# The one-hot blocks of a look-up move from VectorE to GpSimd in a fused attention and look-up FFN kernel

## Chip, cores and metric
One core of one Trainium2 chip. The metric is device time in microseconds for one launch of the whole kernel; lower is better. Comparisons in this document are medians of several executions. A difference of about 0.3% (2.1 us here) is the least that a measurement of this kernel can tell from no change.

## What is computed
Two layers, each an attention and a feed-forward part, with residual additions between them. Cut to what matters here (16 batches of 128 rows by 256 columns):

```
# layer 0, attention: 8 heads of 16, over the 256 columns of x[b]
q      = x[b].T @ Wq.T                       # one projection serves as q, k and v
logits = (scale * q q^T masked by columns) * mask of rows     # mask = cond[b]
ctx    = softmax(logits) @ q ;  out0 = ctx @ Wo.T
# layer 0, FFN: its weights are looked up in a table of 16 values
W      = lut[idx]                            # gate 688x256, up 688x256, down 256x688
h      = silu(out0 @ Wgate.T) * (out0 @ Wup.T) ;  x = x + h @ Wdown.T
# layer 1: attention with 16 heads, then a mixture of 4 experts, one expert per row
```

Everything that the change touches lies in the first attention (the first 220 us or so) and in the look-up of the weights `W`, which the kernel does alongside it.

## The kernel before
The kernel is written engine by engine: each engine has its own instruction stream, and semaphores order them. The first attention runs one batch at a time in a software pipeline. In "body i" TensorE (PE) computes the scores of batch i, the transposed scores and contexts of batch i - 1, and the output projection of batch i - 2. Bodies run from 1 to 15 (`LAST`); bodies 3 to 14 are in hardware loops, two bodies to one pass.

The steps of body i that matter:

- **Maxima.** PE writes the scores of a batch in eight pieces into two halves of PSUM bank PB (`scores`, L808). VectorE (DVE) takes the row maxima of each piece (`maximum`, L1231). A piece can be written when the maximum that read its half is done.
- **The turn of the batch.** After the eighth maximum DVE runs `max_columns(i)`: L1238 copies the maxima as bf16 into `mcol`, L1240 writes their low parts (two inputs in SBUF), and L1242 writes the column for absent rows, which doesn't depend on the maxima. PE then transposes `mcol` (`max_rows`, L858), and DVE adds the result to the stacked queries (`add_max`, L1247). PE's transposed scores of the batch (L820) wait for that addition, so nothing of the next body but one piece of scores and one projection can run before it.
- **One-hot blocks.** The look-up is done by matmuls (L847): a block of 32 x 128 indices is spread over 128 partitions by a DMA from `idx_low` (`load_hot`, L544, issued by ScalarE at the start of body i for block i, 1 MB written), compared with each partition's value (`one_hot`, L1220 in the trace, 128x4096 bf16, output again 0 or 1 in bf16), and multiplied by the table. There are 17 blocks (`LCH`). In the kernel before DVE does `one_hot(i - 1)` between `max_columns(i)` and `add_max(i)`. Blocks 15 and 16 have no body of their own and come after body 15; the load of block 16 waits for `one_hot(14)`, and the FFN waits for the last look-up (`w0` reaching `LCH`).
- **Context.** DVE normalises the context of batch i - 2 in four steps, L1253, L1256, L1259 (two inputs in SBUF) and L1266, which signals `ct`. PE projects it (L865), ScalarE copies it out (L534), and GpSimd splits it into high and low bf16 parts (`context_parts`, L381 and L384).
- **GpSimd (POOL).** Once PE has placed batch i + 1 (`pq`), GpSimd makes the product of x and mask for batch i + 2 (`projected`: L389, two inputs, and the copy L391). Then it waits for the context of batch i - 2 and splits it. Between bodies 13 and 14 it issues ten DMAs with weights for the second layer (L426, L427).

Of the kernel before, what the change touches and what calls it, by code (L numbers as in the profile page):

```python
# [10 lines left out]
ALU = mybir.AluOpType  # L11
# [31 lines left out]
LCH = -(-LUSED // LCOLS)  # L43
# [7 lines left out]
ROW_MAX, ROW_MAX_LOW, ROW_ABSENT = 3, 7, 11  # L51
# [3 lines left out]
C_V = C_ROWS + SLOTS  # L55
# [25 lines left out]
def program(nc, x, cond, condT, consts, wqT, woT, lut, idx_all, w_emb, b_emb, g_norm, w_qkv, g_q, g_k,  # L81
            w_out, w_outT, w_r, b_r, w_all, out, tok_x, tok_r, idx_low):
    with ExitStack() as ctx:
        def sb(name, shape, dt=F32):
            return ctx.enter_context(nc.sbuf_tensor(name, shape, dt))
# [8 lines left out]
        cst = sb("cst", [P, C_N])  # L94
# [17 lines left out]
        def bf(*shape):  # L112
            n = int(np.prod(shape)) // 2
            v = arena[:, at[0]:at[0] + n].bitcast(BF16)
            at[0] += n
            return v
# [20 lines left out]
        spread = bf(2, LHOT).rearrange("p (a c) -> p a c", a=2)  # L137
        hot = bf(2, LHOT).rearrange("p (a c) -> p a c", a=2)
# [21 lines left out]
        def part(shape, dt=F32):  # L160
            n = int(np.prod(shape[1:])) * (1 if dt == F32 else 2) // (1 if dt == F32 else 4)
            v = small[:, small_at[0]:small_at[0] + n]
            small_at[0] += n
            assert small_at[0] <= SMALL
            if dt != F32:
                v = v.bitcast(dt)
            names = "abcd"[:len(shape) - 1]
            if len(names) == 1:
                return v
            return v.rearrange(f"p ({' '.join(names)}) -> p {' '.join(names)}", **dict(zip(names, shape[1:])))  # L170
# [15 lines left out]
        nmax = sb("nmax", [P, PAIRS, 2, KT])  # L186
        mcol = part([P, KT, PAIRS, P], BF16)
# [84 lines left out]
        S = {}  # L272
# [17 lines left out]
        def unless_first(engine, semaphore, count):  # L290

            if not (isinstance(count, int) and count <= 0):
                engine.wait_ge(semaphore, count)

        def hot_rows(c):

            return idx_low[:, bass.ds(c * LHOT, LHOT)].unsqueeze(1).broadcast_to([LG, LUT, LHOT])

        block = ctx.enter_context(nc.Block())
        LAST = B - 1  # L300
        U = B // 2
# [69 lines left out]
        def _(pool):  # L371
# [5 lines left out]
            def context_parts(b):  # L377
                pool.wait_ge(S["c"], b + 1)
                o = bass.ds(b * P, P)
                c32 = c_out.rearrange("p (k t) -> p k t", k=KT)  # L380
                nc.gpsimd.tensor_tensor(c_hi[:, :, o], c32, wz[:].unsqueeze(2).broadcast_to([P, KT, P]), ALU.add  # L381
                                        ).then_inc(S["ch"], 1)
                pool.wait_ge(S["ch"], b + 1)
                nc.gpsimd.tensor_tensor(c_lo[:, :, o], c32, c_hi[:, :, o], ALU.subtract).then_inc(S["cl"], 1)  # L384


            def projected(b, par, half):
                pool.wait_ge(S[f"mk{par}"], 16 * half + 16)
                nc.gpsimd.tensor_tensor(xm[:, par, :].unsqueeze(1), xall[:, bass.ds(b, 1), :], mk[:, par, :].unsqueeze(1),  # L389
                                        ALU.mult).then_inc(S["xm"], 1)  # L390
                nc.gpsimd.tensor_copy(present[:, par, :], mk[:, par, :]).then_inc(S["present"], 1)  # L391

            def body(i, par, half, before=True, after=True):
                if after:
                    pool.wait_ge(S["pq"], 2 * i + 2)
                    projected(i + 2, par, half)
                if before:
                    context_parts(i - 2)

            pool.wait_ge(S["x"], 16)  # L400
            projected(0, 0, 0)
            projected(1, 1, 0)
            nc.gpsimd.memset(vu[:], 1.0).then_inc(S["ones"], 1)
            pool.wait_ge(S["idx"], 16)
# [6 lines left out]
            pool.wait_ge(S["idxs"], 16)  # L411
            for c in range(2):
                pool.dma_start(spread[:, c, :], hot_rows(c)).then_inc(S[f"hot_first{c}"], 16)
            body(1, 1, 1, before=False)
            pool.wait_ge(S["x_rest"], 16)
            body(2, 0, 2)
            with pool.Fori(1, U - 2) as u:
                body(2 * u + 1, 1, u + 1)
                body(2 * u + 2, 0, u + 2)
            body(LAST - 2, 1, U - 1)  # L420
            for dst, src in ((wemb[:], w_emb.rearrange("(k p) n -> p k n", p=P)), (bemb[:], b_emb), (gnorm[:], g_norm),
                             (gqk[:, 0, :], g_q.broadcast_to([P, DK1])), (gqk[:, 1, :], g_k.broadcast_to([P, DK1])),
                             (w2[:, :, 0:T], w_out.rearrange("(k p) n -> p k n", p=P)),
# [1 line left out]
                             (wr[:], w_r.rearrange("(k p) n -> p k n", p=P)), (br[:], b_r.broadcast_to([P, E]))):  # L425
                pool.dma_start(dst, src).then_inc(S["small3"], 16)  # L426
            pool.dma_start(wqkv[:], w_qkv.rearrange("(k p) n -> p k n", p=P)).then_inc(S["wqkv"], 16)  # L427
            body(LAST - 1, 0, 0, after=False)
            body(LAST, 1, 0, after=False)
            context_parts(LAST - 1)  # L430
            context_parts(LAST)

# [751 lines left out]
        def _(dve):  # L1184
            v = nc.vector
# [25 lines left out]
                                    ).then_inc(S["lutw"], 1)  # L1211


            def one_hot(c, par, half):
                if isinstance(c, int) and c < 2:
                    dve.wait_ge(S[f"hot_first{c}"], 16)
                else:
                    dve.wait_ge(S[f"hot{par}"], 16 * half)
                unless_first(dve, S["lmm"], c - 1)
                v.tensor_scalar(hot[:, par, :], spread[:, par, :], cst[:, C_V:C_V + 1], None, ALU.is_equal).then_inc(S["onehot"], 1)  # L1220

            def low(b):
                dve.wait_ge(S["ph"], b + 1)
                unless_first(dve, S["pq"], 2 * b)
                v.tensor_tensor(pl[:], PA[:, 0:T], ph[:], ALU.subtract).then_inc(S["pl"], 1)

            def maximum(b, c, s):
                dve.wait_ge(S["sa"], 8 * b + 2 * c + s + 1)
                if c == s == 0:
                    unless_first(dve, S["mc"], 3 * b)  # L1230
                v.tensor_reduce(nmax[:, c, s, :], PB[:, s * 512:(s + 1) * 512].rearrange("p (a k) -> p a k", k=T),  # L1231
                                AX.X, ALU.max, negate=True).then_inc(S["max"], 1)

            def max_columns(b):
                dve.wait_ge(S["max"], 8 * b + 8)
                unless_first(dve, S["mt"], b)
                cols = mcol.rearrange("p q r (s m) -> p r s q m", s=2)
                v.tensor_copy(cols[:, :, :, :, ROW_MAX], nmax[:]).then_inc(S["mc"], 1)  # L1238
                dve.wait_ge(S["mc"], 3 * b + 1)
                v.tensor_tensor(cols[:, :, :, :, ROW_MAX_LOW], nmax[:], cols[:, :, :, :, ROW_MAX], ALU.subtract).then_inc(S["mc"], 1)  # L1240

                v.tensor_copy(mcol[:, :, :, ROW_ABSENT::64].rearrange("p q r s -> p q (r s)"),  # L1242
                              nbig[:, :, bass.ds(b, 1)].broadcast_to([P, KT, 2 * PAIRS])).then_inc(S["mc"], 1)

            def add_max(b, par):
                dve.wait_ge(S["mt"], b + 1)
                v.tensor_tensor(qs[:, par, :], PD[:, 512:1024].bitcast(BF16), qs[:, par, :], ALU.add).then_inc(S["q2"], 1)  # L1247
# [20 lines left out]
            def body(i, par, half, before=True, after=True):  # L1268
                if before:
                    normalise(i - 2, 0)  # L1270
                maximum(i, 0, 0)
                if before:
                    normalise(i - 2, 1)
                    normalise(i - 2, 2)
                maximum(i, 0, 1)
                if before:
                    normalise(i - 2, 3)
                if after:
                    low(i + 1)
                maximum(i, 1, 0)  # L1280
                maximum(i, 1, 1)
                maximum(i, 2, 0)
                maximum(i, 2, 1)
                maximum(i, 3, 0)
                maximum(i, 3, 1)
                max_columns(i)
                one_hot(i - 1, 1 - par, half)
                add_max(i, par)

            dve.wait_ge(S["kprep"], 1)  # L1290
            low(0)
            low(1)
            for c in range(4):
                for s in range(2):
                    maximum(0, c, s)
            max_columns(0)
            add_max(0, 0)
            table()
            body(1, 1, 0, before=False)
            body(2, 0, 0)  # L1300
            with dve.Fori(1, U - 1) as u:
                body(2 * u + 1, 1, u)
                body(2 * u + 2, 0, u)
            body(LAST, 1, U - 1, after=False)
            for n in range(4):
                normalise(LAST - 1, n)
            for c in range(LAST, LCH):
                one_hot(c, c % 2, c // 2)
            for n in range(4):
                normalise(LAST, n)  # L1310

# [384 lines left out]
```

## Time and profile before

| | us |
|---|---|
| median of 3 runs | 706.95 |
| lowest and highest | 706.39 and 708.73 |
| the profiled execution | 707.92 |
| its span in the trace | 706.2 |

| engine | busy in the span |
|---|---|
| TensorE matmul | 580.7 us, 82% |
| VectorE | 419.2 us, 59% |
| ScalarE | 326.3 us, 46% |
| GpSimd | 118.9 us, 17% |

Durations in the trace come from the one profiled execution, which took 0.97 us more than the median. Busy shares are means over stages with different limits; within the first attention DVE is busy for most of each batch and GpSimd for about a fifth of it.

### The profile page before, as it was taken

What the parts mean: (1) busy time and instruction counts of PE and PEld (TensorE: products, weight loads), DVE (VectorE), ACT (ScalarE), POOL (GpSimd) and SP (SyncE); (2) the same over time, 40 slices, a digit from 0 to 9 for tenths busy, and PEclk for the clock granted to TensorE, in tenths of its full rate; (3) what the DMA queues carried; (4) which work ended last, traced back from release to release, by engine and by line L of the source; (5) the groups of instructions that cost most, each with busy time, mean ns of one, the idle gap of its engine ahead of it and who ended that gap; (6) DMA issues with size and microseconds to landing.
All of it is one profiled execution on the core that took longest, in us unless ns stands there. A gap on an engine that the chain in (4) does not pass through costs nothing.

```text
span 706.2 us, 15569 instructions
## 1 busy us (share of the span) xinstructions
PE 580.7 (82%) x5115; PEld 347.5 (49%) x5147; DVE 419.2 (59%) x943; ACT 326.3 (46%) x592; POOL 118.9 (17%) x161
## 2 busy tenths in 40 slices
PE   3798989899976999995688777775199999999992
PEld 1344445455534655552354554443156666666661
DVE  1678698989853334343799999996523333333330
ACT  2456667677752332342677777773022222222220
POOL 4221122121511000000000000000203333322211
PEclk9999899999986999997799999997599999999996
DMA  8844345454851000005556666551101111011110
GB/s 295 202 95 113 90 110 123 113 121 108 156 134 32 1 1 0 0 0 125 159 120 150 149 147 148 132 137 46 24 22 46 45 45 41 31 37 37 45 32 3
DMA packets 29413, 60.27 MB, mean 85 GB/s; under 512 B 5989, under 2 KB 16647, under 8 KB 26952
## 3 DMA queue, kind: packets, MB, share of 16 engines
q1 hardware_dynamic: 20624, 25.68, 12.4%
q0 software_dynamic: 6432, 18.46, 12.2%
q10 hardware_dynamic: 2328, 15.75, 9.6%
q8 instruction: 18, 0.29, 0.2%
q14 instruction: 11, 0.09, 0.0%
HBM read 58.75 MB, written 7.81 MB: 94 GB/s over the span
## 4 chain that ended last, share of the span: by engine, by line
PE 27%; DVE 14%; issue 7%; ACT 3%; DVEq 1%; DMA 0%; POOL 0%; POOLq 0%; ACTq 0%
PE PA L1134 8%; PE PD L1153 7%; PE PB L1134 7%; PE PC L1142 2%; DVE arena L1479 2%; DVE small L1451 1%; ACT small L661 1%; DVE ms L1405 1%; DVE newt L1373 1%; PE PB L1020 1%; DVE rs L1379 1%; DVE newt L1376 1%; DVE small L1433 1%; DVE small L1437 1%; PE PD L1122 1%
## 5 line engine op out<-in xcount | busy, mean ns | idle before, releaser
L1231 DVE TENSOR_REDUCE nmax<-PB 128x2 f32<-128x512 f32 x128 | 85.5, 681 | 27.0 <-PE PB L808 25.4
L529 ACT ACTIVATE probs<-PC 128x512 f32<-128x512 f32 x128 | 73.9, 609 | 21.6 <-PE PC L820 20.6
L737 ACT CAST probs<-PC 128x1024 bf16<-128x1024 f32 x19 | 19.2, 1012 | 113.7 <-PE PC L1142 113.7
L1625 DVE TENSOR_TENSOR probs<-PC,probs 128x1024 bf16<-128x1024 f32 x19 | 23.3, 1225 | 80.9 <-ACT probs L737 80.9
L1134 PE MATMUL PA<-arena,probs 128*128 x227 | 53.7, 387 | 7.6 <-issue 3.8
L808 PE MATMUL PB<-small 64*128 64x256 bf16 x256 | 52.4, 297 | 8.2 <-DVE nmax L1231 6.1
L1153 PE MATMUL PD<-arena,probs 128*128 x456 | 54.5, 277 | 2.5 <-issue 2.5
L820 PE MATMUL PC<-small 64*128 64x256 bf16 x256 | 48.1, 289 | 3.8 <-DVE small L1247 3.5
L1153 PEld LDWEIGHTS PD<-arena,probs 128*128 128x128 bf16 x456 | 45.0, 99 | 9.0 <-issue 3.2
L1134 PE MATMUL PB<-arena,probs 128*128 x210 | 48.6, 379 | 0.9
L444 POOL DMA_DIRECT2D arena<-in_w_all x16 | 8.5, 532 | 236.7 <-DVE arena L1479 139.5
L669 ACT ACTIVATE probs<-PA,gb 128x1024 f32<-128x1024 f32 x32 | 35.6, 1113 | 14.7 <-PE PA L1047 14.7
L834 PE MATMUL PD<-probs,vu 128*32 128x256 f32 x512 | 38.6, 424 | 4.5 <-ACT probs L529 2.4
L1134 PEld LDWEIGHTS PA<-arena,probs 128*128 128x128 bf16 x228 | 22.4, 99 | 34.8 <-issue 14.5
L466 POOL DMA_INDIRECT out<-probs,tokn x19 | 19.3, 1016 | 118.2 <-DVE probs L1632 118.2
L1348 DVE TENSOR_TENSOR wst<-PB,wst 128x512 f32<-128x512 f32 (+1 forms) x24 | 16.6, 690 | 34.8 <-PE PB L972 26.5
L972 PE MATMUL PA<-arena 128*128 (+1 forms) x133 | 34.2, 389 | 1.9 <-ACT arena L539 1.1
L1020 PE MATMUL PB<-wqkv,small 128*128 128x512 f32 x64 | 34.0, 657 | 2.1 <-ACT small L640 2.1
L972 PE MATMUL PB<-arena 128*128 (+1 forms) x143 | 35.4, 382 | 0.1
L1134 PEld LDWEIGHTS PB<-arena,probs 128*128 128x128 bf16 x228 | 22.3, 98 | 22.9
L1479 DVE TENSOR_TENSOR arena<-wst,arena 128x512 f32 (+1 forms) x48 | 32.6, 682 | 0.0
L381 POOL TENSOR_TENSOR arena<-wst,wz 128x256 f32 (+1 forms) x16 | 9.8, 613 | 133.5 <-ACT wst L534 133.5
(201 smaller groups left out, 1163.9 us busy)
## 6 DMA issues: line engine op xcount, KB each, us to landing
arena<-idx_low ACTq DMA_DIRECT2D x15, 1024.0 KB
wst<-in_w_all SPq DMA_DIRECT2D x48, 256.0 KB, 2.7
arena<-in_w_all POOLq DMA_DIRECT2D x16, 384.0 KB, 5.9
arena<-in_idx_all SPq DMA_DIRECT2D x1, 2176.0 KB, 10.1
arena<-in_cond SPq DMA_DIRECT2D x16, 128.0 KB, 9.3
small<-in_x SPq DMA_DIRECT2D x16, 128.0 KB, 10.0
arena<-idx_low POOLq DMA_DIRECT2D x2, 1024.0 KB, 14.9
tok_r<-rows SPq DMA_DIRECT2D x1, 2048.0 KB, 14.4
```

What stands on the lines that cost most here:

```text
L529: nc.scalar.activation(probs[:, c, o], PC[:, o], ACT.Exp, scale=SCALE0).then_inc(S["ex"], 1)
L669: nc.scalar.activation(probs[:, 2 * par + c, :], PA[:], ACT.Exp, scale=DK1 ** -0.5, bias=gb[:]).then_inc(S["e3"], 1)
L808: ins = mm(PB[:, s * 512 + qt * T:s * 512 + (qt + 1) * T], qs[r, par, c * T + qt * P:c * T + (qt + 1) * P], ks[r, par, c * T:(c + 1) * T], ...
L820: ins = mm(PC[:, s * 512 + n * T:s * 512 + (n + 1) * T], ks[r, par, pr * T + kt * P:pr * T + (kt + 1) * P], qs[r, par, pr * T:(pr + 1) * T ...
L834: ins = mm(PD[h * HS:(h + 1) * HS, pp * T:(pp + 1) * T], vu[:, par, kt, GROUP * pp + h, :], probs[:, pp * KT + kt, o:o + T], start=(kt == ...
L972: ins = mm(o, w0(w, which, kt, m), v[:, kt, tok], start=(k == 0), stop=(k == 3 * KT - 1))
L1020: ins = mm(PB[:, 0:512], xnT[:, kt, :], wqkv[:, kt, 0:512], start=(kt == 0), stop=(kt == KT - 1))
L1134: ins = mm(bank[:, n * 512:(n + 1) * 512], v[:, par, xo], w[:, o], start=(k == 0), stop=(k == 3 * KT - 1))
L1153: ins = mm(PD[:, 512:512 + T], v[:, f * P:(f + 1) * P], w[:, o], start=(k == 0), stop=(k == 3 * FT - 1))
L1231: v.tensor_reduce(nmax[:, c, s, :], PB[:, s * 512:(s + 1) * 512].rearrange("p (a k) -> p a k", k=T), AX.X, ALU.max, negate=True).then_inc( ...
L1479: v.tensor_tensor(all_lo[:, o], wst[:, n, par * SUB:(par + 1) * SUB], all_hi[:, o], ALU.subtract).then_inc(S[f"wsl{n}"], 1)
L1625: v.tensor_tensor(hT_lo, PC[:], hT_hi, ALU.subtract).then_inc(S["hTl"], 1)
```

## The change
`one_hot` moves from DVE to GpSimd. In body i GpSimd now first waits for the loaded block i - 1 and for `ct` of batch i - 2 (the end of DVE's normalising in this body); then it makes `projected(i + 2)`, then `one_hot(i - 1)`, then `context_parts(i - 2)`. Blocks 15 and 16 are made by GpSimd too, ahead of the last two `context_parts`. On DVE the copy for absent rows moves ahead of the eighth maximum (which moves into `max_columns`), and `add_max` follows `max_columns` directly. The comparison itself, its operands and its size stay the same.

```diff
+            def hot_ready(c, par, half):
+                if isinstance(c, int) and c < 2:
+                    pool.wait_ge(S[f"hot_first{c}"], 16)
+                else:
+                    pool.wait_ge(S[f"hot{par}"], 16 * half)
+                unless_first(pool, S["lmm"], c - 1)
+            def one_hot(c, par):
+                nc.gpsimd.tensor_scalar(hot[:, par, :], spread[:, par, :], cst[:, C_V:C_V + 1], None, ALU.is_equal).then_inc(S["onehot"], 1)
...
-            def body(i, par, half, before=True, after=True):
+            def body(i, par, half, hot, before=True, after=True):
+                hot_ready(i - 1, 1 - par, hot)
+                if before:
+                    pool.wait_ge(S["ct"], i - 1)
                 if after:
                     pool.wait_ge(S["pq"], 2 * i + 2)
                     projected(i + 2, par, half)
+                one_hot(i - 1, 1 - par)
                 if before:
                     context_parts(i - 2)
...
+            for c in range(LAST, LCH):
+                hot_ready(c, c % 2, c // 2)
+                one_hot(c, c % 2)
             context_parts(LAST - 1)
             context_parts(LAST)
...
             def max_columns(b):
-                dve.wait_ge(S["max"], 8 * b + 8)
+                cols = mcol.rearrange("p q r (s m) -> p r s q m", s=2)
                 unless_first(dve, S["mt"], b)
-                cols = mcol.rearrange("p q r (s m) -> p r s q m", s=2)
-                v.tensor_copy(cols[:, :, :, :, ROW_MAX], nmax[:]).then_inc(S["mc"], 1)
-                dve.wait_ge(S["mc"], 3 * b + 1)
-                v.tensor_tensor(cols[:, :, :, :, ROW_MAX_LOW], nmax[:], cols[:, :, :, :, ROW_MAX], ALU.subtract).then_inc(S["mc"], 1)
-
                 v.tensor_copy(mcol[:, :, :, ROW_ABSENT::64].rearrange("p q r s -> p q (r s)"),
                               nbig[:, :, bass.ds(b, 1)].broadcast_to([P, KT, 2 * PAIRS])).then_inc(S["mc"], 1)
+                maximum(b, 3, 1)
+                dve.wait_ge(S["max"], 8 * b + 8)
+                v.tensor_copy(cols[:, :, :, :, ROW_MAX], nmax[:]).then_inc(S["mc"], 1)
+                dve.wait_ge(S["mc"], 3 * b + 2)
+                v.tensor_tensor(cols[:, :, :, :, ROW_MAX_LOW], nmax[:], cols[:, :, :, :, ROW_MAX], ALU.subtract).then_inc(S["mc"], 1)
...
                 maximum(i, 3, 0)
-                maximum(i, 3, 1)
                 max_columns(i)
-                one_hot(i - 1, 1 - par, half)
                 add_max(i, par)
...
             for n in range(4):
                 normalise(LAST - 1, n)
-            for c in range(LAST, LCH):
-                one_hot(c, c % 2, c // 2)
             for n in range(4):
                 normalise(LAST, n)
```

## Rows read from the trace of the kernel before

**Rows 1.** Timeline, turn of batch 10: start us, duration us, engine, line, operation, [idle before]

```profile
144.67 0.69 DVE L1231 TENSOR_REDUCE nmax<-PB 128x2 f32<-128x512 f32 x1 [0.74 <-PE PB L808]
...
145.37 1.07 PE L834 MATMUL PD<-probs,vu 128*32 128x256 f32 x16
145.40 0.20 DVE L1238 CAST small<-nmax 128x16 bf16<-128x16 f32 x1
145.60 0.73 POOL L389 TENSOR_TENSOR small<-arena 128x256 f32<-128x256 f32 x1 [0.87 <-PE PA L792]
145.64 0.77 DVE L1240 TENSOR_TENSOR small<-nmax,small 128x16 bf16<-128x16 f32 x1
...
146.27 0.40 POOL L391 CAST arena<-arena 128x256 bf16<-128x256 f32 x1
146.29 0.43 DVE L1242 CAST small<-nbig 128x16 bf16 x1
146.61 1.27 DVE L1220 TENSOR_SCALAR arena<-arena,cst 128x4096 bf16<-128x4096 bf16 x1
146.78 0.62 PE L858 MATMUL PD<-identb,small 128*128 128x128 bf16 x8 [0.34 <-DVE small L1242]
...
147.81 0.68 DVE L1247 TENSOR_TENSOR small<-PD,small 128x1024 bf16<-128x1024 bf16 x1
```

**Rows 2.** Timeline, the part of body 10 ahead of that turn

```profile
136.51 0.68 DVE L1247 TENSOR_TENSOR small<-PD,small 128x1024 bf16<-128x1024 bf16 x1
...
139.53 0.44 DVE L1266 STREAM_TRANSPOSE wst<-small 128x256 f32<-128x256 f32 x1
...
142.42 1.51 DVE L1231 TENSOR_REDUCE nmax<-PB 128x2 f32<-128x512 f32 x2 [0.28 <-PE PB L808]
...
143.25 0.61 POOL L381 TENSOR_TENSOR arena<-wst,wz 128x256 f32 x1 [7.87 <-ACT wst L534]
```

**Rows 3.** Timeline, turn of batch 15, with no GpSimd work beside it

```profile
199.93 1.07 PE L834 MATMUL PD<-probs,vu 128*32 128x256 f32 x16 [0.88 <-ACT probs L529]
...
200.94 0.62 PE L858 MATMUL PD<-identb,small 128*128 128x128 bf16 x8
...
201.59 0.69 DVE L1247 TENSOR_TENSOR small<-PD,small 128x1024 bf16<-128x1024 bf16 x1
```

**Rows 4.** GpSimd by line: shapes, count | busy us, mean ns | idle before, releasers

```profile
L384 POOL TENSOR_TENSOR arena<-wst,arena 128x256 f32 (+1 forms) x16 | 10.7, 671 | 2.4 <-POOL arena L381 1.9
L381 POOL TENSOR_TENSOR arena<-wst,wz 128x256 f32 (+1 forms) x16 | 9.8, 613 | 133.5 <-ACT wst L534 133.5
...
L391 POOL CAST arena<-arena 128x256 bf16<-128x256 f32 x16 | 6.4, 399 | 0.0
L405 POOL CAST arena<-arena 128x4352 bf16<-128x4352 int32 x1 | 3.8, 3811 | 3.6 <-DMA arena<-in_idx_all 3.6
```

**Rows 5.** Timeline, turn of batch 0

```profile
23.97 0.41 DVE L1238 CAST small<-nmax 128x16 bf16<-128x16 f32 x1
...
25.61 1.01 PE L858 MATMUL PD<-identb,small 128*128 128x128 bf16 x8 [2.41 <-DVE small L1242]
```

**Rows 6.** Line L413, loads of blocks 0 and 1: duration min/median/max, first and last start

```profile
L413 POOL DMA_DIRECT2D arena<-idx_low x2: 613/650/687, 23.0 to 23.7; - x2
...
DMA to landing us min/median/max: 13.7/14.9/16.1
```

**Rows 7.** One batch: window, length, busy PE, PEld, DVE, ACT, POOL, clock, DMA share, GB/s

```profile
64.22:80.31 16.09, 14.40 (x137) 7.34 (x137) 10.32 (x19) 8.41 (x16) 2.36 (x4) 0.68 0.35 89
```

**Rows 8.** Timeline, end of the first attention and the last blocks

```profile
178.12 0.80 POOL L426 DMA_DIRECT2D wemb<-in_w_emb  x1
...
180.97 0.64 ACTq L544 DMA_DIRECT2D arena<-idx_low  x1
...
217.69 1.29 DVE L1220 TENSOR_SCALAR arena<-arena,cst 128x4096 bf16<-128x4096 bf16 x1 [7.39 <-DMA arena<-idx_low]
...
219.04 1.02 PE L847 MATMUL PD<-lutw,arena 128*128 128x16 bf16 x32 [4.49 <-DVE arena L1220]
```

More of the change, by code:

```diff
@@ L396, in body @@
                     projected(i + 2, par, half)
+                one_hot(i - 1, 1 - par)
                 if before:
                     context_parts(i - 2)
+            pool.wait_ge(S["cst"], 16)
             pool.wait_ge(S["x"], 16)
@@ L413, in _ @@
                 pool.dma_start(spread[:, c, :], hot_rows(c)).then_inc(S[f"hot_first{c}"], 16)
-            body(1, 1, 1, before=False)
+            body(1, 1, 1, 0, before=False)
             pool.wait_ge(S["x_rest"], 16)
-            body(2, 0, 2)
+            body(2, 0, 2, 0)
             with pool.Fori(1, U - 2) as u:
-                body(2 * u + 1, 1, u + 1)
-                body(2 * u + 2, 0, u + 2)
-            body(LAST - 2, 1, U - 1)
+                body(2 * u + 1, 1, u + 1, u)
+                body(2 * u + 2, 0, u + 2, u)
+            body(LAST - 2, 1, U - 1, U - 2)
             for dst, src in ((wemb[:], w_emb.rearrange("(k p) n -> p k n", p=P)), (bemb[:], b_emb), (gnorm[:], g_norm),
@@ L427, in _ @@
             pool.dma_start(wqkv[:], w_qkv.rearrange("(k p) n -> p k n", p=P)).then_inc(S["wqkv"], 16)
-            body(LAST - 1, 0, 0, after=False)
-            body(LAST, 1, 0, after=False)
+            body(LAST - 1, 0, 0, U - 2, after=False)
+            body(LAST, 1, 0, U - 1, after=False)
+            for c in range(LAST, LCH):
+                hot_ready(c, c % 2, c // 2)
+                one_hot(c, c % 2)
             context_parts(LAST - 1)
@@ L1211, in table @@
                                     ).then_inc(S["lutw"], 1)
[L1214 to L1220, printed above, removed]
             def low(b):
@@ L1292, in _ @@
             low(1)
-            for c in range(4):
-                for s in range(2):
-                    maximum(0, c, s)
+            for n in range(7):
+                maximum(0, n // 2, n % 2)
             max_columns(0)
```

## The prediction, made before the changed kernel was run
> **What bounds the kernel now.** I read the timeline of one ordinary batch first, since the busy shares don't say which wait ends last. Body 10 runs from one `add_max` to the next, 136.51 to 147.81, 11.30 us [rows 1, 2]; below, t counts from its start. DVE is nearly always busy, but idles 0.74 us ahead of the eighth maximum, waiting for PE [rows 1]. After that maximum (t = 8.16 to 8.85) comes a chain of single steps: L1238, L1240, L1242, PE's `max_rows` at 146.78 (t = 10.27), and `add_max` at t = 11.30.
>
> Two costs sit in this chain. **First**, L1240 and L1242, 16 elements each, take 0.77 and 0.43 us. L1240 ends just after GpSimd's L389 ends (146.41 and 146.33), L1242 just after L391 ends (146.72 and 146.67): DVE stands still while GpSimd works, and gets in as each GpSimd instruction ends [rows 1]. **Second**, `one_hot` on DVE ends at 147.88, so `add_max` starts 1.03 us after `max_rows` did; where nothing stands in the way it starts 0.65 us after it (200.94 to 201.59) [rows 1, 3].
>
> PE sets a floor under both. `max_rows` stands behind 16 context matmuls, which hold PE's queue for 1.01 us (199.93 to 200.94) [rows 3]. In body 10 they start at t = 8.86 [rows 1], so `max_rows` can't start before t = 9.87, nor `add_max` before 10.52. At most 0.8 us of 11.30 is to be had, not the 1.27 us of the removed instruction. Bodies 13 to 15 have no products of x and mask and nearly stand there: block 14's load, issued as body 14 starts, and `add_max` of batch 15 are two batches and 20.6 us apart [rows 3, 8].
>
> **What the moved comparison costs on GpSimd.** No row shows it. The nearest are GpSimd's one-input casts: 128x256 in 0.399 us, 128x4352 in 3.811 us [rows 4], which is 3.412 / 4096 = 0.833 ns an element and 0.19 us fixed. For 4096 elements: 3.6 us. The other end is the two-input rows: L381 (613 - 186) / 256 = 1.67 ns an element, so 7.0 us; L384 (671 - 186) / 256 = 1.89 ns, so 7.9 us [rows 4]. Below 1.27 us, DVE's own time [rows 1], I exclude. I take 3.6: the comparison has one input in columns (the other is one value a partition), as the casts do, and L405 has almost its length.
>
> **The body after.** GpSimd now waits for `ct`, the end of L1266 at t = 3.46 [rows 2], plus 0.19, what L384 waits for L381 (1.9 us over 10) [rows 4]. Behind that wait stand the products, the comparison and the split of the context. The products take 0.73 and 0.40 us, overlapping by 0.06 [rows 1]: t = 3.65 to 4.7. PE wants them only in the next body, and SP's next mask load only half a body later, so this delay costs nothing. The comparison runs t = 4.7 to 8.3. L381 and L384 follow, 0.61, 0.19 and 0.67 us: to t = 9.8 (before they began at t = 6.74 [rows 2]). ScalarE needs that buffer again a batch later: no cost.
>
> DVE meets this in two places. L1242, now ahead of the eighth maximum, is due at t = 7.42 (142.42 + 1.51) [rows 2]; without contention it would hide in the 0.74 us of idling. The comparison holds it to 8.3, so the eighth maximum starts at 8.35 instead of 8.16 and ends at 9.05. Then L1238 and L1240 (0.20 and 0.23 us free) meet L384, t = 9.1 to 9.8: whichever goes first, L1240 ends near 10.0. `max_rows` starts at 10.1 and `add_max` 0.65 later, 10.75. Against 11.30 (its neighbours are about 11.2) that is **0.5 us a batch**, where the floor allows 0.8.
>
> **The sum.** Turns 2 to 12 have the products beside them now: 11 x 0.5 = 5.5 us, of which I give batch 4, at a lower clock, the same. Turn 0: L1238 ends at 24.38; with L389 and L391 waiting for block 0, `max_rows` starts at 24.38 + 0.04 + 0.23 + 0.06 = 24.7 instead of 25.61: 0.9 us [rows 5]. Block 0 lands near 23.0 + 13.7 = 36.7 [rows 6], its comparison then runs from 37.8 to 41.4, and the turn of batch 1 falls there; I take L1238 and L1240 as just ahead of it, at nothing; if they lose, 2 us. Body 13 loses 0.3 us (10.75 instead of 10.4). So body 14 begins 0.9 + 5.5 - 0.3 = 6.1 us earlier, and load 14 with it.
>
> Now the end. Block 16's comparison waited 7.39 us for its DMA, until 217.69, and the last look-up follows at 219.04 [rows 8]; the FFN waits for that. The stream of loads 14 to 16, mixed with the ten weight DMAs that GpSimd issues from 178.12, sets the end, not the engines. Load 14 (180.97) leaves 6.1 us earlier. The weight DMAs stand behind body 13's comparison and leave 2 us later within their body (t = 9.8 instead of 7.8), so 6.4 - 2.0 = 4.4 us earlier. With both kinds sharing the DMA engines the last block lands between: 5.3 us earlier. In body 14 the comparison stands behind the ten issues and holds the turn by some 2 us; that cover is the same DMA wait. At the end the comparison of block 16 takes 3.6 - 1.3 = 2.3 us longer with nothing beside it. Net 5.3 - 2.3 = **3.0 us**. The profiled execution (707.92, of which 706.2 is span) would be 704.9; it is 0.97 above the median, so 706.95 - 3.0 = **703.9 us**.
>
> A rule of the Trainium skill speaks of the stall: "SBUF — State Buffer", section "Who interferes with whom", says that a GpSimd instruction and a VectorE instruction with two SBUF inputs or in a two-port mode exclude each other for the whole instruction. The trace agrees, with 0.77 us for 16 elements [rows 1]. By it L1242 would be held up to 3.6 us if it came as the comparison started, while the maxima, which read PSUM, would run on.
>
> **Rivals.**
>
> *The comparison is slow on GpSimd, and DVE waits for it (slower).* If it runs at the two-input rate, 7.0 us, it ends at t = 11.7; L1242 and with it the eighth maximum are held until then, and `add_max` comes 2.45 us after its end, as in my reckoning (8.3 to 10.75), at t = 14.15. Each us above 3.6 costs 1 us in each of bodies 2 to 13 and about half of one at the end, 12.5 in all. It decides from 3.6 + 3.0 / 12.5 = 3.84 us: slower beyond that, and measurably from 4.0. At 5 us the time is 703.9 + 17.5 = 721.4, at 7.0 us 703.9 + 42.5 = 746.4. For it: no row shows a comparison on GpSimd, and two-input rows are twice as slow an element. Against: the one-input casts of two types and lengths lie on one line. "GPSIMD Engine Reference" of the Trainium skill, section 7, points the same way as this rival: loops that compare and then select need 2.03 cycles an element unless unrolled, 1.03 if they are; at its 1.2 GHz an estimate of 6.9 us or 3.5 us.
>
> *The gain is lost at the end (no change).* If the weight DMAs alone decide when block 16 lands, and turn 1 loses its race with block 0's comparison (2 us), what is left is 4.4 - 2.0 - 2.3 = 0.1 us: 706.9. For it: the tail already waits for DMAs, and any gain of the batches has to pass them. Against: load 14 is issued with the batch, not by GpSimd.
>
> *Batch 4 keeps its clock (faster still).* That batch takes 16.09 us with a granted clock of 0.68, partly at 1.2 instead of 2.4 GHz, against 11.3 for others [rows 7]. If the new timing spares it that drop, 4.8 us more come off: 699.1. The same chance cuts the other way if a drop comes elsewhere.
>
> **How the numbers follow.** My forecast 0.50 (its own range 701.5 to 706.5, by the races at the turns and the DMA mix; of it 0.36 are faster by over 0.3%, about what a measurement of this kernel can tell from no change). Slow comparison 0.28, nearly all slower. Lost at the end 0.12, mostly no change. The clock 0.10, mostly faster. That gives faster 0.44, same 0.23, slower 0.33. The range runs from 699 to 722: below it little is left, above it the comparison over 5 us, 0.15 or so.
>
> **What would show it.** The comparison's row on GpSimd, near 3.6 us, decides most. L1242 should end with the comparison, near t = 8.3; L1240 should end near 10.0, `max_rows` should follow at 10.1 and `add_max` 0.65 later; the batches should be 10.7 to 10.8 us apart. The last comparison should start near 212.4 and the last look-up near 216.1. I am wrong if the comparison is longer than 3.8 us, if DVE's instructions lose more than one race a turn, or if block 16 lands less than 4 us earlier.

## The result: 14.5% slower, and the profile after

The changed kernel takes 806.66 us (median of 4 runs, 802.85 to 812.12) against 706.67 us; the ratio is 1.145, 95% interval 1.139 to 1.151. Its profiled execution took 812.12 us, of which 810.0 is span. Each later experiment has runs of the kernel before made beside it: 29 with a median of 707.34 (702.25 to 711.99) for the experiments 1 to 3, 7 with 707.71 for 5 and 6, and 11 with 707.74 for 4 and for the repeated run in 3. A ratio leaves out executions over 1.5% above the fastest of their kernel, which are two of the ten in experiment 2 and none elsewhere.

Nearly all of it lies in the first attention: the last look-up starts at 317.41 instead of 219.04 [rows 8], 98.4 us later, of 103.8 between the two spans. The other 5.4 us lie behind it, in an execution that was itself 5.5 above the median of its kernel. The two costliest groups there, from the page of the changed kernel (line engine op, shapes, count | busy us, mean ns | idle before), and its row of granted clock in 40 slices:

```profile
L394 POOL TENSOR_SCALAR arena<-arena,cst 128x4096 bf16<-128x4096 bf16 x17 | 180.6, 10624 | 4.9 <-DVE wst L1275 4.9
...
L1246 DVE CAST small<-nbig 128x16 bf16 (+1 forms) x16 | 79.6, 4978 | 0.0
...
PEclk9998555686566565999997799999856999999997
```

The comparison takes **10.62 us** on GpSimd, where VectorE took 1.27 [rows 1]. And a copy of 16 elements, L1246 (L1242 before), takes 4.98 us in the mean. The timeline of body 7 shows how they belong together; it answers to [rows 1, 2]. (`add_max` is L1256 now, the maxima L1240, the end of normalising L1275, the two steps behind the eighth maximum L1250 and L1252.)

```profile
138.38 0.69 DVE L1256 TENSOR_TENSOR small<-PD,small 128x1024 bf16<-128x1024 bf16 x1 [1.13 <-PE PD L875]
...
141.64 0.44 DVE L1275 STREAM_TRANSPOSE wst<-small 128x256 f32<-128x256 f32 x1
...
142.52 0.73 POOL L398 TENSOR_TENSOR small<-arena 128x256 f32<-128x256 f32 x1 [4.74 <-DVE wst L1275]
...
143.57 10.63 POOL L394 TENSOR_SCALAR arena<-arena,cst 128x4096 bf16<-128x4096 bf16 x1
143.57 0.69 DVE L1240 TENSOR_REDUCE nmax<-PB 128x2 f32<-128x512 f32 x1 [0.17 <-PE PB L825]
...
148.99 5.26 DVE L1246 CAST small<-nbig 128x16 bf16 x1
...
152.41 1.85 DVE L1240 TENSOR_REDUCE nmax<-PB 128x2 f32<-128x512 f32 x1
154.17 0.62 POOL L381 TENSOR_TENSOR arena<-wst,wz 128x256 f32 x1
154.32 0.53 DVE L1250 CAST small<-nmax 128x16 bf16<-128x16 f32 x1
...
154.88 0.23 DVE L1252 TENSOR_TENSOR small<-nmax,small 128x16 bf16<-128x16 f32 x1
...
155.17 0.62 PE L875 MATMUL PD<-identb,small 128*128 128x128 bf16 x8 [3.09 <-DVE small L1252]
...
155.82 0.69 DVE L1256 TENSOR_TENSOR small<-PD,small 128x1024 bf16<-128x1024 bf16 x1 [0.71 <-PE PD L875]
```

What is to be seen: the comparison runs from 143.57 to 154.20, that is t = 5.2 to 15.8. L1246 starts at 148.99 and ends at 154.25, 0.05 us after the comparison, though it has 16 elements a partition. The next `add_max` follows at t = 17.44, against 11.30 before. In most batches it is 17.88: there TensorE, which now idles for about 3 us in a turn, has fallen to its 1.2 GHz level, and `max_rows` lasts 1.03 instead of 0.62 us. The maximum behind L1246 has a record of 1.85 us that overlaps with L1246 and ends within 0.01 us of it. So the time of the maximum did not come on top of the wait.

Where the 98.4 us are, by the starts of `add_max` in both traces: the turn of batch 1 comes 7.3 us later (48.74 against 41.46; the first two rows below), batches 2 to 11 add 60.1 (226.42 against 159.02), batches 12 to 15 add 28.4 (297.38 against 201.59), and the end 2.6. There two comparisons run back to back, and the last look-up waits for GpSimd instead of for the DMA [rows 8]:

```profile
38.63 10.62 POOL L394 TENSOR_SCALAR arena<-arena,cst 128x4096 bf16<-128x4096 bf16 x1
38.73 8.88 DVE L1252 TENSOR_TENSOR small<-nmax,small 128x16 bf16<-128x16 f32 x1
...
284.23 10.61 POOL L394 TENSOR_SCALAR arena<-arena,cst 128x4096 bf16<-128x4096 bf16 x1 [4.88 <-DVE wst L1275]
...
296.15 21.20 POOL L394 TENSOR_SCALAR arena<-arena,cst 128x4096 bf16<-128x4096 bf16 x2
...
317.41 1.02 PE L864 MATMUL PD<-lutw,arena 128*128 128x16 bf16 x32 [1.57 <-POOL arena L394]
```

### The profile page after: what moved, and what is told of

It reads as the page before. It is cut to its first block and busy times, and to the rows that moved or that the text cites. A ratio compares the mean times of both kernels' runs of the same rounds, so it can differ in the third digit from the quotient of the medians.

```text
span 810.0 us, 15559 instructions
## 1 busy us (share of the span) xinstructions
PE 645.8 (80%) x5115; PEld 371.6 (46%) x5147; DVE 484.7 (60%) x926; ACT 333.5 (41%) x592; POOL 297.2 (37%) x178
## 5 line engine op out<-in xcount | busy, mean ns | idle before, releaser
L394 POOL TENSOR_SCALAR arena<-arena,cst 128x4096 bf16<-128x4096 bf16 x17 | 180.6, 10624 | 4.9 <-DVE wst L1275 4.9
L1240 DVE TENSOR_REDUCE nmax<-PB 128x2 f32<-128x512 f32 x128 | 103.3, 812 | 47.2 <-PE PB L825 45.4
L1246 DVE CAST small<-nbig 128x16 bf16 (+1 forms) x16 | 79.6, 4978 | 0.0
L825 PE MATMUL PB<-small 64*128 64x256 bf16 x256 | 71.6, 387 | 1.3 <-DVE nmax L1240 1.3
L837 PE MATMUL PC<-small 64*128 64x256 bf16 x256 | 62.7, 387 | 1.0 <-DVE small L1256 1.0
L875 PE MATMUL PD<-identb,small 128*128 128x128 bf16 x128 | 15.3, 293 | 52.4 <-DVE small L1252 52.4
L851 PE MATMUL PD<-probs,vu 128*32 128x256 f32 x512 | 49.8, 526 | 4.4 <-ACT probs L546 2.4
L523 ACT CAST ph<-PA 128x256 bf16<-128x256 f32 x16 | 6.0, 372 | 93.7 <-PE PA L788 88.1
L686 ACT ACTIVATE probs<-PA,gb 128x1024 f32<-128x1024 f32 x32 | 35.6, 1113 | 15.3 <-PE PA L1064 15.3
L875 PEld LDWEIGHTS PD<-identb,small 128*128 128x128 bf16 x128 | 11.4, 132 | 61.6 <-DVE small L1252 59.7
L398 POOL TENSOR_TENSOR small<-arena 128x256 f32<-128x256 f32 x16 | 11.7, 730 | 73.3 <-DVE wst L1275 54.4
```

The source lines that it names most:

```text
L394: nc.gpsimd.tensor_scalar(hot[:, par, :], spread[:, par, :], cst[:, C_V:C_V + 1], None, ALU.is_equal).then_inc(S["onehot"], 1)
L686: nc.scalar.activation(probs[:, 2 * par + c, :], PA[:], ACT.Exp, scale=DK1 ** -0.5, bias=gb[:]).then_inc(S["e3"], 1)
L825: ins = mm(PB[:, s * 512 + qt * T:s * 512 + (qt + 1) * T], qs[r, par, c * T + qt * P:c * T + (qt + 1) * P], ks[r, par, c * T:(c + 1) * T], ...
L837: ins = mm(PC[:, s * 512 + n * T:s * 512 + (n + 1) * T], ks[r, par, pr * T + kt * P:pr * T + (kt + 1) * P], qs[r, par, pr * T:(pr + 1) * T ...
L851: ins = mm(PD[h * HS:(h + 1) * HS, pp * T:(pp + 1) * T], vu[:, par, kt, GROUP * pp + h, :], probs[:, pp * KT + kt, o:o + T], start=(kt == ...
L875: ins = pe.transpose(M[:, pr * T + qt * P:pr * T + (qt + 1) * P], mcol[:, qt, pr, :], identb[:])
```

## Experiment 1: what makes the comparison so slow

Behind the last store of the kernel before, GpSimd runs nine operations one after the other, each waiting for the one ahead. (A step that fills the f32 inputs with ones comes first and isn't shown.) `cv` is the column of one value a partition.

```diff
+step(g.tensor_scalar(hot[:, 0, :], spread[:, 0, :], cv, None, ALU.is_equal))
+step(g.tensor_scalar(hot[:, 0, 0:2048], spread[:, 0, 0:2048], cv, None, ALU.is_equal))
+step(g.tensor_scalar(hot[:, 0, 0:1024], spread[:, 0, 0:1024], 3.0, None, ALU.is_equal))
+step(g.tensor_scalar(hot[:, 0, 0:512], spread[:, 0, 0:512], cv, None, ALU.mult))
+step(g.tensor_scalar(fout[:, 0:2048], fin[:, 0:2048], cv, None, ALU.is_equal))
+step(g.tensor_copy(hot[:, 0, :], spread[:, 0, :]))
+step(g.tensor_tensor(hot[:, 0, 0:1536], spread[:, 0, 0:1536], spread[:, 1, 0:1536], ALU.mult))
+step(g.tensor_tensor(fout[:, 0:1536], fin[:, 0:1536], fin[:, 1536:3072], ALU.mult))
+step(g.tensor_scalar(fout[:, 0:1792], fin[:, 0:1792], cv, None, ALU.mult))
```

> The kernel before, with ten GpSimd instructions added one after the other behind its last store: the moved comparison again (4096 columns of bf16), the same at 2048, the comparison against a constant (1024), a multiplication by the same column of cst (512 bf16, 1792 f32), the comparison in f32 (2048), a plain copy (4096 bf16) and two-input products (1536 bf16, 1536 f32). Theory A, the comparison itself is slow: it takes 2.5 to 2.6 ns an element at every size, type and kind of scalar, the multiplications by a column and the copy stay at the cast's 0.83. Theory B, any instruction with a scalar is slow on GpSimd: the multiplications take 2.5 ns too. Theory C, bf16 is slow: the f32 comparison is at 0.83 and the bf16 copy at 2.5. The time is some 30 to 45 us above that of before and of no interest.

Timeline of that run, GpSimd alone:

```profile
701.04 10.64 POOL L500 TENSOR_SCALAR arena<-arena,cst 128x4096 bf16<-128x4096 bf16 x1
711.77 5.43 POOL L501 TENSOR_SCALAR arena<-arena,cst 128x2048 bf16<-128x2048 bf16 x1
717.29 2.77 POOL L502 TENSOR_SCALAR arena<-arena 128x1024 bf16<-128x1024 bf16 x1
720.16 1.58 POOL L503 TENSOR_SCALAR arena<-arena,cst 128x512 bf16<-128x512 bf16 x1
721.83 5.44 POOL L504 TENSOR_SCALAR arena<-arena,cst 128x2048 f32<-128x2048 f32 x1
727.34 3.60 POOL L505 COPY arena<-arena 128x4096 bf16<-128x4096 bf16 x1
731.02 3.08 POOL L506 TENSOR_TENSOR arena<-arena 128x1536 bf16<-128x1536 bf16 x1
734.18 3.42 POOL L507 TENSOR_TENSOR arena<-arena 128x1536 f32<-128x1536 f32 x1
737.69 4.80 POOL L508 TENSOR_SCALAR arena<-arena,cst 128x1792 f32<-128x1792 f32 x1
```

**Theory B holds.** It is one execution, but each instruction starts within 0.1 us of the end of the one ahead, so the starts give the same lengths. From 4096 and 2048 columns: 5.21 / 2048 = 2.54 ns an element and 0.22 us fixed. A multiplication (512 and 1792 columns), an immediate in place of the column (1024), and f32 all lie on that line within 0.1 us. The plain copy of the same 4096 elements takes 3.60 us, exactly what the prediction took for the comparison. So the kind of instruction sets the rate: the operations with a scalar that were tried (is_equal and a product) cost GpSimd three times a copy an element, and more than a product of two tensors (1.9 to 2.1 ns, with the copy's fixed 0.19 us taken off). "GPSIMD Engine Reference" of the Trainium skill, section 4.1, calls one-input operations on GpSimd roughly line rate. The copy agrees (0.83 ns), the operation with a scalar doesn't; the measurement decides. That comparing is what costs, which section 7 would have suggested, is refuted: the multiplication is as slow.

## Experiment 2: the same design with the cost that was predicted

```diff
-nc.gpsimd.tensor_scalar(hot[:, par, :], spread[:, par, :], ...)
+nc.gpsimd.tensor_scalar(hot[:, par, 0:1344], spread[:, par, 0:1344], ...)
```

The blocks are also set to zero once at the start (not shown). Everything beyond column 1344 is left out, so this kernel computes something else and serves only for its time.

> The changed kernel with the comparison cut to its first 1344 of 4096 columns (the other columns of the blocks stay zero, so most of the looked-up weights are left out); the look-up's matmuls and all waits are as they were. At 2.55 ns an element it takes 3.6 us, what the prediction took for the whole. Theory 1, only the size of that term was wrong: 703.9 (701.5 to 706.5), batches 10.7 to 10.8 us apart, add_max some 2.45 us after the end of the comparison. Theory 2, a comparison beside VectorE costs more than its length, by the exclusion of each other's SBUF accesses: above 707, batches over 11.3 us apart.

Measured: 707.4 us (10 runs, 699.87 to 711.88), ratio 0.998 (0.994 to 1.002). The comparison takes 3.69 us. Timeline of body 9 of this run:

```profile
120.66 0.69 DVE L1258 TENSOR_TENSOR small<-PD,small 128x1024 bf16<-128x1024 bf16 x1 [0.93 <-PE PD L877]
...
125.63 3.69 POOL L395 TENSOR_SCALAR arena<-arena,cst 128x1344 bf16<-128x1344 bf16 x1
...
128.01 1.37 DVE L1248 CAST small<-nbig 128x16 bf16 x1
128.76 0.69 DVE L1242 TENSOR_REDUCE nmax<-PB 128x2 f32<-128x512 f32 x1
...
130.45 0.62 PE L877 MATMUL PD<-identb,small 128*128 128x128 bf16 x8
...
131.11 0.69 DVE L1258 TENSOR_TENSOR small<-PD,small 128x1024 bf16<-128x1024 bf16 x1 [0.87 <-PE PD L877]
```

Inside the first attention theory 1 holds in that the comparison costs no more than its length, and the batch is even shorter than forecast: 10.45 and 10.52 us in turn instead of 10.75, TensorE's floor. `add_max` follows 1.8 us behind the comparison (129.32 to 131.11), not 2.45. The copy (here L1248) is held to 129.38, but the maximum behind it starts at 128.76 as soon as TensorE has the scores. The FFN's first matmul (of the group in PA) starts 5.7 us earlier than before (215.42 against 221.14). Yet the whole is not faster, and as a time both theories missed: 707.4 lies above the range of the one, and its batches are far below those of the other. In the profiled execution all but 1.2 us of the gain is gone within 45 us of the start of the FFN, whose granted clock is lower (columns as in [rows 7]; the kernel before has 0.90 and 1.00 in its first two such windows):

```profile
214.00:234.00 20.00, 18.87 (x106) 11.07 (x106) 6.71 (x19) 5.89 (x9) 3.10 (x5) 0.77 0.01 1
234.00:254.00 20.00, 18.48 (x102) 10.12 (x102) 6.94 (x12) 5.35 (x9) 0.00 (x0) 0.91 0.01 1
```

The kernels of experiments 3 and 4 keep their gain. Why this one doesn't was not settled. That most of its looked-up weights are zero is not enough for it: in experiment 4 a kernel with nearly all of them zero keeps its gain, with a granted clock of 0.89 and 1.00 in the same two stretches of its FFN (207 to 227 and 227 to 247).

## Experiment 3: the second part of the change by itself

The change also delays the products of x and mask until VectorE has normalised the context. Here that alone, with the comparison left on VectorE, and then with the new order of the copy as well.

```diff
             def body(i, par, half, before=True, after=True):
+                if before:
+                    pool.wait_ge(S["ct"], i - 1)
                 if after:
                     pool.wait_ge(S["pq"], 2 * i + 2)
                     projected(i + 2, par, half)
```

> The kernel before with one wait added: GpSimd makes the products of x and mask only after ct, as in the changed kernel; the comparison stays on VectorE. Theory 1, L1240 and L1242 stand still for the products: they fall to 0.23 and 0.20 us in all turns, add_max comes 0.7 us earlier in 11 of them, and the time is 699 (698 to 701). Theory 2, the floor of TensorE and the comparison on VectorE eat it: 705 to 707.

Measured: 700.39 us (12 runs, 695.74 to 705.58), ratio 0.990 (0.987 to 0.993). Timeline of a turn of this run:

```profile
140.81 0.68 DVE L1249 TENSOR_TENSOR small<-PD,small 128x1024 bf16<-128x1024 bf16 x1
...
149.63 0.21 DVE L1240 CAST small<-nmax 128x16 bf16<-128x16 f32 x1
149.87 0.23 DVE L1242 TENSOR_TENSOR small<-nmax,small 128x16 bf16<-128x16 f32 x1
149.97 0.21 DVE L1244 CAST small<-nbig 128x16 bf16 x1
150.16 1.29 DVE L1222 TENSOR_SCALAR arena<-arena,cst 128x4096 bf16<-128x4096 bf16 x1
151.37 0.68 DVE L1249 TENSOR_TENSOR small<-PD,small 128x1024 bf16<-128x1024 bf16 x1
```

The two small steps take 0.23 and 0.21 instead of 0.77 and 0.43 us [rows 1], and the batch 10.56 us (140.81 to 151.37) instead of 11.30. Theory 1 holds: **the gain that the prediction ascribed to the change is real, and is that of one wait.** With the order of `max_columns` as in the changed kernel in addition:

> The same, and the copy for absent rows ahead of the eighth maximum, as in the changed kernel; the comparison stays on VectorE. It takes that copy off the chain, so the comparison starts 0.1 us earlier behind L1240. Theory 1: 0.1 us a turn more than with the wait alone, 1 to 2 us in all, 697.5 to 699. Theory 2, the copy was hidden behind L1240 anyway: within 0.5 us of the run with the wait alone.

Measured: 700.26 us (12 runs), ratio 0.992 (0.988 to 0.995); batches 10.45 and 10.52 us apart in turn, where the wait alone has 10.54 and 10.56. So the trace has 0.06 us a batch of the 0.1 that theory 1 gave, and the time is theory 2's: it can't be told from the run with the wait alone. It was repeated beside later runs:

> The kernel with later products and the new order again, as the measure for the two above on the same chip: 699 to 702, and 0.988 to 0.995 of the kernel before.

Measured: 699.74 us (6 runs), ratio 0.988 (0.983 to 0.993).

## Experiment 4: is there more to be had from moving the comparison?

First the most that any place for it could give: VectorE compares 64 columns of 4096.

```diff
-v.tensor_scalar(hot[:, par, :], spread[:, par, :], ...)
+v.tensor_scalar(hot[:, par, 0:64], spread[:, par, 0:64], ...)
```

(To the kernel with the wait and the new order; the blocks are set to zero once, not shown.)

> The kernel of the run with later products and the new order, with VectorE's comparison cut to 64 of 4096 columns (the rest stays zero, so nearly all of the looked-up weights is left out) and none on GpSimd: the most that any placing of the comparison can give. Theory 1, TensorE's floor (context matmuls, max_rows, add_max: 10.5 us a batch) already sets that kernel: batches stay 10.45 to 10.55 us apart, and the time is within 2 us of 700.3, except for 1.2 us that the last comparison is shorter. Theory 2, the comparison on VectorE still costs: batches under 10.3 us apart, 694 to 697.

Measured: 696.91 us (6 runs), ratio 0.984 (0.980 to 0.988). In the trace theory 1 holds: batches are 10.45 and 10.53 us apart in turn, as with the whole comparison on VectorE, which now waits for `max_rows` as long as it had compared before:

```profile
128.29 0.24 DVE L1224 TENSOR_SCALAR arena<-arena,cst 128x64 bf16<-128x64 bf16 x1
129.47 0.69 DVE L1251 TENSOR_TENSOR small<-PD,small 128x1024 bf16<-128x1024 bf16 x1 [0.94 <-PE PD L861]
```

As a time 696.91 lies at the edge of both theories. It is 2.8 us below the 699.74 of the repeated run of experiment 3, made beside it. Of these, 1.05 us are the last comparison, 0.24 instead of 1.29 us; the rest is within the spread of the runs, as the two intervals of the ratio overlap. It is no gain per batch, since the batches are the same. Then the comparison shared, with both engines in their gaps:

```diff
 (in the changed kernel)
+nc.gpsimd.tensor_scalar(hot[:, par, 0:1024], spread[:, par, 0:1024], ...)
+v.tensor_scalar(hot[:, par, 1024:], spread[:, par, 1024:], ...)   # between max_columns and add_max
```

> The changed kernel with the comparison shared: GpSimd makes the first 1024 columns (0.24 + 1024 x 2.53 ns = 2.8 us, done at t = 7.5, just about when the copy for absent rows is due), VectorE the other 3072 behind L1252, about 1.0 us. Theory 1, both then lie in gaps and the floor sets the batch: 10.5 us apart, 699 to 702, the same as with the comparison left on VectorE. Theory 2, sharing costs by itself: batches over 10.7 us apart, 703 or more.

Measured: 700.99 us (6 runs, 699.92 to 702.52), ratio 0.990 (0.987 to 0.994), batches 10.46 to 10.52 us apart: theory 1. The copy behind GpSimd's 2.86 us loses 0.35 us and it doesn't matter:

```profile
136.10 2.86 POOL L394 TENSOR_SCALAR arena<-arena,cst 128x1024 bf16<-128x1024 bf16 x1
...
138.46 0.55 DVE L1256 CAST small<-nbig 128x16 bf16 x1
```

So taking the comparison off VectorE gains nothing per batch, and nothing that these times can tell, in part or nearly in whole. The best kernel with all its data is the one with the wait, with or without the new order.

## Experiment 5: VectorE shut out, or GpSimd full?

```diff
-nc.gpsimd.tensor_scalar(hot[:, par, :], spread[:, par, :], ...).then_inc(S["onehot"], 1)
+for k in range(8):
+    o = slice(k * LHOT // 8, (k + 1) * LHOT // 8)
+    ins = nc.gpsimd.tensor_scalar(hot[:, par, o], spread[:, par, o], ...)
+ins.then_inc(S["onehot"], 1)
```

> The changed kernel with the comparison as eight instructions of 512 columns, each about 0.24 + 512 x 2.53 ns = 1.5 us, 12.3 us in all, so that VectorE can get in between them. Theory 1, all of the loss is VectorE being shut out for one long instruction: each of L1246, L1250 and L1252 waits 1.5 us at most, batches are 12 to 12.5 us apart, 715 to 725. Theory 2, GpSimd's own work is a bound by itself as well: products 1.07, comparison 12.3, split of the context 1.5 and the wait for ct make 15.1 us a batch, against 17.9 in the changed kernel, so the time is 806.7 - 13 x 2.8 = 770 (760 to 780), with VectorE idle for other reasons than its accesses. Theory 3, neither: it stays at 800 or more.

Measured: 786.88 us (4 runs), ratio 1.112 (1.103 to 1.121). VectorE is held for about 1 us a turn at most, and still most of the loss stays (a timeline, then the window of batches 3 to 11, columns as in [rows 7]):

```profile
129.13 12.34 POOL L396 TENSOR_SCALAR arena<-arena,cst 128x512 bf16<-128x512 bf16 x8
...
135.01 0.37 DVE L1249 CAST small<-nbig 128x16 bf16 x1
...
64.00:200.00 136.00, 115.82 (x1209) 58.94 (x1208) 80.45 (x155) 73.53 (x144) 129.02 (x107) 0.76 0.35 87
```

GpSimd is busy for 129.0 of 136.0 us: it has become the bound by itself. Theory 2 named the mechanism, and batches 3 to 11 take 15.1 us in the mean (63.74 to 199.24), as it said. Its 770 us were too low, since batch 2 took 24.2 us and batches 12 to 15 took 16.4 in the mean. So of the 100 us at least 20 go to VectorE being shut out. How many exactly this run doesn't show, since the pieces also made GpSimd's own work longer, 12.34 us a block instead of 10.63. By an estimate, 17 blocks x 1.7 us = 29 us more would be gone without that, so VectorE's waiting and GpSimd's own work would each be worth about half.

## Experiment 6: the price of length, and of the clock

The comparison at 2688 columns, 7.08 us:

> The changed kernel with the comparison cut to 2688 of 4096 columns (the others stay zero, so part of the looked-up weights is left out), about 7.05 us. The recorded rival's price for 7.0 us is 746.4, at 12.5 us of time for each us of comparison. Theory 1, the price holds: 742 to 751. Theory 2, the straight line between the runs at 1344 columns (707.4) and at 4096 (806.7), 14.2 us for each us: 753 to 759, because the lower clock adds to it.

Measured: 752.69 us (4 runs, 751.1 to 753.54), ratio 1.064 (1.056 to 1.073). A step of 3.39 us from 3.69 cost 45.3 us, 13.4 for each us; the next, of 3.54 us to 10.62, cost 54.0, or 15.3 for each. These prices are 7% and 22% above the prediction's 12.5. The time lies between the ranges of the two theories, 1.7 us above the first and 0.3 below the second. The base of 707.4 holds the loss in the FFN that was not settled, so the first price is read better from the batches: they grew from 10.49 to 13.75 us, 0.96 for each us, and then to 17.88, 1.17 for each. The granted clock between 85 and 225 us is 0.82 here and 0.62 in the changed kernel.

Can the clock be had back? The changed kernel with matmuls ahead of `max_rows` of batches 2 to 15 (abridged):

```diff
             def max_rows(b):
+                for _ in range(14):
+                    mm(PD[:, 512:1024], identb[:], sel[...512 columns...], start=True, stop=True)
                 pe.wait_ge(S["mc"], 3 * b + 3)
```

> The changed kernel with 14 matmuls of 512 columns with no use added for TensorE ahead of max_rows of batches 2 to 15, 3.0 us at full clock, in the 3.1 us in which it otherwise waits for VectorE; nothing reads them. Theory 1, the lower clock that follows TensorE's idling costs 0.9 us a batch (the wait for ct ends 0.5 us later in the batch, and max_rows takes 0.4 us longer): granted clock over 0.9 in the first attention, 792 to 798. Theory 2, VectorE and GpSimd set the batch whatever the clock: 803 to 808.

Measured: 806.55 us (4 runs), ratio 1.139 (1.129 to 1.148): theory 2 by the time. The granted clock between 85 and 225 us rose from 0.62 to 0.85, and batches at full clock are 17.2 us apart instead of 17.9. But in two batches the clock was low all the same (0.50 up to 134.38 in body 6). There the added matmuls started only when the comparison had ended, took 4.1 and 4.0 us instead of 3.2, and `max_rows` stood behind them: 19.8 us. This shows a price of the clock of about 0.65 us a batch, and no way to save it. VectorE stands still the longer for coming earlier:

```profile
143.90 10.62 POOL L394 TENSOR_SCALAR arena<-arena,cst 128x4096 bf16<-128x4096 bf16 x1
...
146.29 8.29 DVE L1249 CAST small<-nbig 128x16 bf16 x1
```

Last, the copy for absent rows put back behind the step with two inputs:

```diff
-                maximum(i, 3, 0)
-                max_columns(i)      # copy for absent rows, maximum(i, 3, 1), two steps
+                maximum(i, 3, 0)
+                maximum(i, 3, 1)
+                max_columns(i)      # two steps, copy for absent rows
```

> The changed kernel with the copy for absent rows back behind L1252, as in the kernel before; the comparison stays on GpSimd. Theory 1, with so long a comparison the moved copy does harm: it holds the eighth maximum too, so that 0.7 us of maximum stand behind the comparison instead of ahead of it; with the old order 0.5 us a batch come back, 799 to 802. Theory 2, the order makes no difference: 804 to 809.

Measured: 801.09 us (4 runs), ratio 1.133 (1.124 to 1.142). That is 5.6 us less than the changed kernel, as theory 1 said in number, though the interval overlaps with the changed kernel's 1.139 to 1.151, so the step is not clear of noise. Its reason is not borne out. The copy of the maxima takes the place of L1246 and is likewise held to the end of the comparison:

```profile
141.93 10.62 POOL L394 TENSOR_SCALAR arena<-arena,cst 128x4096 bf16<-128x4096 bf16 x1
...
149.43 3.18 DVE L1247 CAST small<-nmax 128x16 bf16<-128x16 f32 x1
152.65 0.58 DVE L1249 TENSOR_TENSOR small<-nmax,small 128x16 bf16<-128x16 f32 x1
```

From the end of the comparison to `add_max` it is 1.46 us (152.55 to 154.01), against 1.62 in the changed kernel: 0.16, not 0.7. In the profiled execution the rest comes with a granted clock of 0.70 instead of 0.62 between 85 and 225 us; why the clock was higher was not tried.

## Why the prediction was wrong

- **What bounds the kernel: right.** The two small steps stood still for the products, `one_hot` held `add_max`, and TensorE's floor is 10.5 us: every changed run without a long comparison on GpSimd has batches 5 to 12 between 10.45 and 10.56, even with VectorE's comparison nearly gone.
- **"What the moved comparison costs on GpSimd": the step that failed.** I took 3.6 us from the casts and 7.9 as the upper end from the two-input rows; it is 10.62. An instruction with a scalar was in no row of GpSimd, and I carried the rate of another kind over to it because the number of inputs was the same. The two-input rows were no bound either: it is slower than they are.
- **The body after: right in order, off in two sizes.** GpSimd's products, comparison and split stand in the order in which they were put, and L1246 ends with the comparison. But `add_max` follows 1.6 to 1.8 us behind the comparison, not 2.45, as the maximum doesn't come on top of the held copy. With the cost that I had assumed the batch is 10.5 us, not 10.75. The comparison starts at t = 5.0 in experiment 2 and 5.2 in the changed kernel, not 4.7: GpSimd's product comes 0.44 us after the end of normalising, where I had put 0.19, and the rest is the lower clock.
- **The turn of batch 0: the size was right, the sum not.** From the end of the eighth maximum to `max_rows` it took 0.65 us instead of 1.68, so 1.0 less, where I had 0.9. But the scores ahead of it came 1.2 us later, which was not looked into, and `add_max` started at 26.90 instead of 26.66.
- **The race of batch 1: lost, and dearer.** I had put it at nothing, 2 us if lost. L1252 starts 0.1 us behind the comparison there and is held for 8.88 us; the turn comes 7.3 us later, as TensorE had contexts to compute in the first part of the wait.
- **The rival "the comparison is slow on GpSimd" had the mechanism,** and by its price of 12.5 us for each us of comparison 10.62 us would have been 703.9 + 87.8 = 791.7. Of the 98.4 us in the trace this price gives 84.8. The turns of batches 0 and 1 cost 8.2 more than it says. Batches 14 and 15 and the end cost 10.3 more, where I had counted on cover by a DMA wait that was gone. Batches 2 to 13 cost 4.8 less, as the 16.09 us of batch 4 [rows 7] were no longer above the others. I gave this rival 0.28, but left a comparison of over 5 us, for which I had 0.15, outside the range, so that it ended at 722.
- **The end: half right.** In the run with the assumed cost the FFN started 5.7 us earlier, more than my 3.0, and that kernel as a whole was still no faster. The kernel with the wait alone carried 8.4 us through to the FFN and 7 to the end.
- **The rival of the lower clock had the wrong sign.** I gave it mostly to a drop that vanishes and named one elsewhere only in passing. Now most batches had one, with TensorE waiting for 3 us in the turn; filling that wait raised the clock from 0.62 to 0.85 (experiment 6).

## What to carry to other kernels

Before moving an operation to GpSimd, time that very kind of instruction there, in one run with a few sizes; another kind's rate an element was off threefold here, with the same inputs, types and length. If two engines exclude each other, first try to move the short instructions in time: one wait gave all of the gain that these runs can tell (0.990), with nothing moved. And work out the floor of the third engine first: it said that at most 0.8 us a batch was to be had, against a risk that was open above. Last, sum up GpSimd's own work for one batch, here 10.6 us of comparison and 2.5 of the rest: it was over the 11.2 us of a batch even if nobody waited for it.

## What the runs showed of the hardware

- GpSimd, 128 partitions (experiment 1, one execution): operation with a scalar 0.22 us + 2.54 ns an element, for is_equal (bf16 and f32, column; bf16, immediate) and mult (bf16 and f32, column), each within 0.1 us; copy 3.60 us for 4096; product of two tensors 3.08 us (bf16) and 3.42 us (f32) for 1536.
- A VectorE copy of 16 elements in SBUF waits for the whole rest of a GpSimd instruction (5.26 us in body 7, up to 10.18 in the run with the added matmuls) and ends 0.05 to 0.06 us after it, not after GpSimd's next one. The step with two inputs is held too (8.88 us in batch 1), but there it ended 1.64 us ahead of the comparison (47.61 against 49.25), which was not explained.
- It goes the other way as well: in the kernel before, the product in the turn of batch 1 (L389 at 38.74) took 1.71 us instead of 0.73 on GpSimd; VectorE's `one_hot` had started 0.15 us ahead of it and ran to 39.87.
- VectorE's maxima from PSUM run beside GpSimd's comparison at 0.69 us (143.57 in body 7). One that stands behind a held copy ended with it and not 0.69 us later.
